# A seven-stage kernel: clearing moved into attention, an early move in the experts stage, free PSUM banks passed on one by one

## The reference, cut to what matters

```
x = x + _layernorm(_L0_attn_ref(_layernorm(x), w_attn, w_proj))          # causal softmax attention, 16 heads of 16
x = x + _layernorm(_L0_ffn_ref(_layernorm(x), ...))                       # 64 experts, 6 a token, at most 96 tokens an expert
x = x + _layernorm(_L1_attn_ref(_layernorm(x), W_qkv, b_qkv, ...))        # linear attention
x = x + _layernorm(_L1_ffn_ref(_layernorm(x), ...))                       # 8 experts, 4 a token, and a shared one

# in _L0_ffn_ref: each expert takes its first CAP = 96 tokens, the rest are dropped
hmid = gelu(einsum('ech,ehf->ecf', xs, w1))
y = einsum('ecf,efh->ech', hmid, w2)
out = zeros((t, h)).at[token_of].add(y_pair)                              # sums over a token's experts
shared = gelu(x @ sw1.T) @ sw2.T
return out + shared

# in _L1_attn_ref, the features of queries and keys
q = elu(q * E ** -0.5) + EPS_FEAT                                         # EPS_FEAT = 1.0001
k = elu(k) + EPS_FEAT
```

## Time and profile before

| | us |
|---|---|
| median of 3 runs | 3391.13 (3386.59 to 3397.05) |
| the profiled execution | 3387.51 |
| its span, first to last instruction | 3385.8 |
| PE busy | 2875.2 (85%) |
| DVE busy | 2228.2 (66%) |
| ACT busy | 1606.3 (47%) |
| POOL busy | 734.7 (22%) |

### The profile page before, as it was taken

The page is one execution under the profiler, slowest core; times in us unless marked ns, Lnnn a source line. Parts: engine busy times, 40 slices in busy tenths (PEclk is TensorE's granted clock), DMA queues, the critical chain, the costliest instruction groups (busy, mean ns, idle before and its releaser), DMA issues. The chain is left out here.

```text
span 3385.8 us, 58986 instructions
## 1 busy us (share of the span) xinstructions
PE 2875.2 (85%) x19969; PEld 2070.7 (61%) x19969; DVE 2228.2 (66%) x6153; ACT 1606.3 (47%) x2398; POOL 734.7 (22%) x876
## 2 busy tenths in 40 slices
PE   6767999999999577574983776999489999999998
PEld 5653444444444266464773664556378888888887
DVE  5448999999999278555335884444366666666664
ACT  2222777777777444331323553455234444444443
POOL 0011222222222133243773441222100000000000
PEclk9886999999999766587996887899689999999999
DMA  6776565656553278684976997554324342425241
GB/s 178 225 209 90 90 99 91 89 85 96 95 92 63 74 251 287 216 332 110 228 185 196 290 288 238 159 174 149 137 72 116 72 116 70 117 69 118 67 102 44
DMA packets 423046, 489.02 MB, mean 144 GB/s; under 512 B 92112, under 2 KB 309232, under 8 KB 420592
## 3 DMA queue, kind: packets, MB, share of 16 engines
q1 hardware_dynamic: 409856, 453.74, 51.6%
q0 software_dynamic: 10240, 14.16, 2.4%
q10 hardware_dynamic: 2800, 19.20, 1.5%
HBM read 280.34 MB, written 206.10 MB: 144 GB/s over the span
## 5 line engine op out<-in xcount | busy, mean ns | idle before, releaser
L529 ACT ACTIVATE att_pr<-att_e_ps 128x1024 f32<-128x1024 f32 (+2 forms) x640 | 567.2, 938 | 203.2 <-PE att_e_ps L581 203.2
L557 PE MATMUL att_m_ps<-att_ks,att_qs 63*128 63x512 f32 (+3 forms) x1536 | 466.2, 433 | 41.1 <-PEq L39 32.5
L491 DVE CUSTOM_DVE_ANT_0 att_kept<-att_m_ps,att_causal 128x256 f32<-128x256 f32 (+3 forms) x1024 | 448.5, 488 | 48.6 <-DVEq L39 21.9
L557 PEld LDWEIGHTS att_m_ps<-att_ks,att_qs 63*128 63x128 f32 x1536 | 234.7, 189 | 371.5 <-DVE att_mx L494 148.0
L494 DVE TENSOR_REDUCE att_mx<-att_m_ps 128x1 f32<-128x512 f32 x512 | 323.4, 684 | 21.4 <-PE att_m_ps L557 17.4
L470 POOL TENSOR_SCALAR_AFFINE_SELECT att_pr<-att_pr 128x256 f32<-128x256 f32 (+1 forms) x384 | 181.2, 484 | 698.0 <-PEq L572 694.5
L601 PE MATMUL att_o_ps<-att_pr,att_vs 128*32 128x512 f32 (+3 forms) x3072 | 328.7, 501 | 3.7 <-issue 1.9
L2574 ACT ACTIVATE fin_hh<-fin_hid 128x512 fp32r<-128x512 f32 x192 | 121.4, 632 | 400.4 <-DVE fin_hid L2420 299.7
L581 PE MATMUL att_e_ps<-att_qs,att_ks 64*128 64x512 f32 (+3 forms) x1536 | 269.4, 377 | 4.8 <-ACT att_pr L529 2.9
L2313 POOL TENSOR_TENSOR fin_rs<-fin_ve,fin_mhalf 128x4 f32<-128x4 f32 x48 | 48.4, 1007 | 928.4 <-POOLq L39 928.4
L2416 DVE TENSOR_TENSOR fin_hid<-fin_gate,fin_u_ps 128x512 f32<-128x512 f32 x192 | 131.7, 686 | 138.0 <-ACT fin_gate L2568 82.9
(11 more groups left out here) (331 smaller groups left out, 6966.1 us busy)
## 6 DMA issues: line engine op xcount, KB each, us to landing
fin_raw<-weights SPq DMA_DIRECT2D x32, 1024.0 KB, 12.7
att_qs<-q_high SPq DMA_DIRECT2D x128, 128.0 KB, 5.1
att_ks<-k_high SPq DMA_DIRECT2D x128, 128.0 KB, 6.7
attended<-att_ot SPq DMA_DIRECT2D x64, 256.0 KB, 2.0
moe_w<-w SPq DMA_DIRECT2D x128, 128.0 KB, 3.4
acc<-moe_zero ACTq DMA_DIRECT2D x16, 1024.0 KB, 12.0
lqk_a<-acc SPq DMA_DIRECT2D x32, 512.0 KB, 6.2
attended<-lin_ot SPq DMA_DIRECT2D x32, 512.0 KB, 3.5
```

The source lines that it names most:

```text
L491: e.tensor_tensor_reduce(kept[:, n % MBUF, 0:w], m_ps[:, n % MBUF, 0:w], causal[:, BLK - w:], 1.0, -3e38, ALU.add, ALU.max, mx[:, h, at, q ...
L529: e.activation(out, src, ACT.Exp).then_inc(exp_done, 1)
L557: e.matmul(m_ps[:, (2 * i + n) % MBUF, 0:w], qs[rows, j, p, q * P:(q + 1) * P], ks[rows, j, p, h * BLK:h * BLK + w], start=True, stop=True ...
```

## The change

Five edits, in four stages.

1. First stage: SyncE signals `qk_read` for each bank as soon as that bank's low part is ready, waits for the values, signals `v_read`, and only then issues all eight stores. TensorE waits for one bank at a time.
2. Attention: a block of zeros is filled by GpSimd, and SyncE issues two stores of 256 KB to `acc0` and `acc1` after each group's row; it waits for all of them at the stage's end.
3. Experts stage: ScalarE's 16 clearing stores are gone, only the three small ones for the dummy rows stay. The small move is issued after 16 pieces and not after 44. VectorE splits the second weight behind `pack()` and not before it.
4. Experts stage, pairs: VectorE's `low` for a pair's second and later pieces comes behind the next pair's `xt` copy.
5. Input of linear attention: `phi = max(qk + bias + 1.0001, min(ex, 1) + 1e-4)`. `ex` is clamped two banks at a time in SBUF; the step that makes `phi` reads PSUM.

```
@@ phase_qkv, sync
                         j = b[1]
-                        e.wait_ge(ol_ready, 4)
+                        for c in range(4):
+                            e.wait_ge(ol_ready, c + 1)
+                            e.sem_inc(qk_read, 1)
+                        e.wait_ge(vo_ready, 1)
+                        e.sem_inc(v_read, 1)
                         for d, s, c in ((qh_d, oh, 0), (kh_d, oh, 2), (ql_d, ol, 0), (kl_d, ol, 2)):
                             e.dma_start(...).then_inc(stored[j], 16)
-                        e.sem_inc(qk_read, 1)
-                        e.wait_ge(vo_ready, 1)
-                        e.sem_inc(v_read, 1)
@@ phase_qkv, tensor
-                        e.wait_ge(qk_read, 1)
                         for c in range(4):
+                            e.wait_ge(qk_read, c + 1)
@@ phase_softmax_attention
+        ZERO = N // G // P * C
+        zero = ph.sb("zero", [P, ZERO])
+        zero_rows = [d[0:N].rearrange("(g p r) c -> g p (r c)", g=G, p=P) for d in zeroed]
+                def clear(g):
+                    for rows in zero_rows:
+                        e.dma_start(rows[g], zero[:]).then_inc(zeros_stored, 16)
                     if more:
                         row(nxt)
+                    clear(g)
@@ phase_shared_and_experts, sync
-                for k in range(ALONE):
+                for k in range(MOVE):
                     follow(k)
                 e.wait_ge(local_ready, 1)
                 e.dma_start(both[:, 1], val[E0:P]).then_inc(moved, 16)
+                for k in range(MOVE, ALONE):
+                    follow(k)
@@ vector
+                split(0, w1h, w1l, w1f)
                 e.wait_ge(choice_loaded, 32)
                 e.wait_ge(iotas_ready, 2)
                 pack()
+                split(1, w2h, w2l, w2f)
                 largest(val[:], key[:])
...
+                    if n:
+                        for k in pieces(n - 1)[1:]:
+                            low(k)
                     low(ks[0])
-                    low(ks[1])
...
-                    for k in ks[2:]:
-                        low(k)
@@ scalar
                 for k in range(ALONE):
                     follow(k)
-                    if k < 2 * (N // (P * ZR)):
-                        n, a = k // 2, k % 2
-                        e.dma_start(zero_v[a][n], zero[:]).then_inc(zeros_stored, 16)
@@ phase_linear_qkv, vector
-                                begun.append(step.begin(e.tensor_scalar(re[:, k], qk[:, k], bqke[:, k:k + 1], FE,
-                                                                        ALU.add, ALU.max)))
-                                e.scalar_tensor_tensor(phi[:, j, k - 1], ex[:, k - 1], 1.0, re[:, k - 1], ALU.min,
-                                                       ALU.add).then_inc(phi_done, 1)
+                        for half in (slice(0, 2), slice(2, 4)):
+                            e.wait_ge(exp_ready, half.stop)
+                            step(e.tensor_scalar(ex[:, half], ex[:, half], 1.0, FE, ALU.min, ALU.add))
+                            for k in range(half.start, half.stop):
+                                e.scalar_tensor_tensor(phi[:, j, k], qk[:, k], bqk1[:, k:k + 1], ex[:, k], ALU.add,
+                                                       ALU.max).then_inc(phi_done, 1)
```

More of the change, by code:

```diff
@@ L254, in _ @@
             def _(e):
-                e.sem_inc(qk_read, 1)
+                e.sem_inc(qk_read, 4)
                 e.sem_inc(v_read, 1)
@@ L267, in stages @@
                                     (lambda k: xh[:, j, k], lambda k: xl[:, j, k]), KC).then_inc(qk_ready, 1)
-                        take(e, (xl_ready, 1), (qk_read, 1))
+                        take(e, (xl_ready, 1), (qk_read, 4))
                     if a is not None:
@@ L317, in phase_softmax_attention @@
         o_ps = ph.ps("o_ps", [P, BLK])
+        zero_ready = ph.sem("zero_ready")
+        zeros_stored = ph.sem("zeros_stored")
         first_ones = ph.sem("first_ones")
@@ L436, in _ @@
                 row(1)
+                e.wait_ge(zero_ready, 1)
+                clear(0)
                 with e.Fori(0, LOOPS) as i:
@@ L442, in _ @@
                 outputs(G - 1, 1)
+                e.wait_ge(zeros_stored, 16 * len(zeroed) * G)
             @block.gpsimd
@@ L459, in _ @@
                 e.sem_inc(later_ones, 1)
+                step(e.memset(zero[:], 0.0))
+                e.sem_inc(zero_ready, 1)
                 step.close()
@@ L1150, in phase_shared_and_experts @@
     ON_POOL = 6
+    MOVE = 4 * NF
     REST = 2 * NF * NB - ALONE
@@ L1244, in phase_shared_and_experts @@
         sh_v = sh_d.rearrange("(b j t p) c -> b j p t c", j=2, t=TPB, p=P)
-        ZR = 2048 // C
-        zero_v = [d[0:N].rearrange("(n p r) c -> n p (r c)", p=P, r=ZR) for d in accs]
-        ZEROS = 2 * (N // (P * ZR)) + 3
         with nc.Block() as block:
@@ L1361, in unpack, with split @@
                         step(e.scalar_tensor_tensor(left[:], bit[:], -weight, left[:], ALU.mult, ALU.add))
-                for n, (high, low, full) in enumerate(((w1h, w1l, w1f), (w2h, w2l, w2f))):
+                def split(n, high, low, full):
                     e.wait_ge(w_high, n + 1)
@@ L1407, in _ @@
                                         None, ALU.mult).then_inc(scaled, 1)
-                    for k in ks[2:]:
-                        low(k)
+                for k in pieces(PAIRS - 1)[1:]:
+                    low(k)
             @block.scalar
@@ L1528, in phase_linear_qkv @@
         bqk = ph.sb("bqk", [P, 4])
-        bqke = ph.sb("bqke", [P, 4])
+        bqk1 = ph.sb("bqk1", [P, 4])
         bv = ph.sb("bv", [P, C])
@@ L1669, in _ @@
                 step(e.tensor_scalar(bqk[:, 0:2], bqk[:, 0:2], HD ** -0.5, None, ALU.mult))
-                step(e.tensor_scalar(bqke[:], bqk[:], FE, None, ALU.add))
+                step(e.tensor_scalar(bqk1[:], bqk[:], 1.0 + FE, None, ALU.add))
                 e.sem_inc(bias_ready, 1)
@@ L1695, in stages @@
                         j = c[1]
-                        begun = []
-                        for k in range(5):
-                            if k < 4:
-                                e.wait_ge(exp_ready, k + 1)
-                                begun.append(step.begin(e.tensor_scalar(re[:, k], qk[:, k], bqke[:, k:k + 1], FE,
-                                                                        ALU.add, ALU.max)))
-                            if k:
-                                step.done(begun[k - 1])
-                                e.scalar_tensor_tensor(phi[:, j, k - 1], ex[:, k - 1], 1.0, re[:, k - 1], ALU.min,
-                                                       ALU.add).then_inc(phi_done, 1)
+                        for half in (slice(0, 2), slice(2, 4)):
[4 more added lines that the diff above has]
+                                                       ALU.max).then_inc(phi_done, 1)
                         e.wait_ge(v_ready, 1)
```

13 lines of the change are left out of this document (6 added, 7 removed).

## The result

The changed kernel takes 3310.8 us, the median of 4 runs (3300.5 to 3321.1), against 3394.1 before (4 runs): a ratio of 0.9755, interval 0.9716 to 0.9793. The prediction was 3279, with a range to 3310. So the sign was right, the gain is 83 us in place of 115, and the time lies 0.8 us outside the range.

What follows compares the result with a forecast made beforehand. Stages have different limits: a semaphore behind four issues holds the first stage, VectorE's list sets the expert pairs' start. 3387.5 - 51.5 - 0 - 42 - 7 - 8 = 3279.0 us; range 3257 to 3310.

Steps and rivals of the forecast that it cites:

- First stage: First stage: SyncE's earlier bank signals shorten a block from 14.1 to 10.5 us; net -51.5 us, bounds -36.5 and -62.5.
- (c): First stage: transfers take 10.5 us a block, the largest of three near bounds, with 11.0 as upper bound.
- Rival A: First stage: transfers need 11.0 us plus a 1.0 restart, 12.0 a block; gain 29 us, time 3301; chance 0.13.
- The first stage's end: First stage: the last block's stores start after the values copy and not before it, costing 2.5 us.
- Clock: First stage: closing the pauses keeps TensorE's clock fast, mean above 0.95, 9.3 us a block; were it wrong, 11.0.
- Rival B: First stage: the clock does not come back; 11.2 us a block, gain 41 us, time 3289.5; chance 0.13.
- Attention: Attention: the added stores of zeros fit in a hole behind the row; 0 us, at most 42 us slower.
- rival D: Attention: clearing delays the next output, making the kernel slower; at 6 us a group, time 3471; chance 0.02.
- Experts, front: Experts stage before the pairs: clearing removed and move early, so the list is done sooner; -42 us, bounds -36 and -47.
- Rival C: Experts stage, front: the move isn't early, the list ends at 1541.3; gain 18 us, time 3303; chance 0.08.
- Pairs: Expert pairs: copying turned rows earlier returns most of TensorE's 9.7 us of waits; -7 us, bounds 0 and -10.
- Linear input: Input of linear attention: the new phi takes 4.2 us a block, before 5.05; -8 us, bounds 0 and -16.

Runs made afterwards that it cites:

- the wide layout: The changed kernel with values stored in packets of 1088 bytes in place of 272, attention loading from the new places: 3273.6 us, ratio 0.9648.
- the wide packets: The changed kernel with values stored in 1088-byte packets, attention still loading from the old places (only times count): first stage 159.9 us.

## Why the prediction was right or wrong

*First stage: wrong, the one step that decided.* It failed at (c), the transfers. The prediction set three near bounds side by side (9.3 for TensorE, 9.75 for SyncE, 10.5 for transfers) and took the largest. The first is borne out: with one DMA for the values the block is 9.3 us and TensorE is busy throughout. The second fits the 9.6 us of the wide layout, though no run isolates it. The third was 11.8 to 12.2. It called 11.0 us of packet time "the upper bound", since a share of 1 is not the capacity. In the saturated stage the share stands at 1.01 to 1.06, and the packet time of a block is 12.2 to 12.7 us. The values' issues, taken as 4.0 us, were not their cost: the packets went on behind the last issue at a share of 1.38 and 169 GB/s, which stood in the earlier trace rows and was read only as proof that there was room. The Trainium skill's rule on 512 bytes, stated above, would have named the risk: values are stored in pieces of 4 heads x 17 numbers, 272 bytes.

Rival A had the size (12.0 us a block, 3301), but partly by luck. It took the 11.0 us of share as what the engines need and added a restart of 1 us; the packet time was longer than 11.0, and there was no restart, since no microsecond from 40 to 190 us stands empty. Its gain of 29 us is what six profiles give (29.4).

*The first stage's end.* I charged 2.5 us for stores that start later. From TensorE's last matmul to attention's first it took 38.3 and 37.3 us, and 35.7 to 37.9 in the four other profiles of this stage; before, 32.5. That is 3 to 6 us longer. With packets of 544 or 1088 bytes it is 29.3 to 31.6: the same small packets drain there.

*Clock.* The granted clock rose to 0.92 only (40 to 150 us), with pauses before the blocks still there; with no pause it reads 1.00. Rival B described the state, but it was a result of the transfers and not the bound: the wide packets alone brought the clock to 1.00.

*Attention: right*, 0, and rival D had nothing to it: 9.2 us of slack behind the two issues.

*Experts, front: right*, -42 forecast, -43.0 measured: the move 1455.75 - 1397.5 = 58 us after the table's load was issued (61 forecast), the list 95 (96). Port waits cost 4 us where I had 2; the local values being ready 2 us sooner and the move landing in 1.9 us in place of 2.9 made up for it. The rule that I had named from the Trainium skill ("SBUF — State Buffer", section "Who interferes with whom") held, with 1.25 us against 0.20. Rival C's case, a late move, is what the run with the move undone shows: a gain of 22 us in place of 18.

*Pairs: wrong*, -7 forecast, +2 in the first profile, -1 in the mean and none by the run with the order undone. The step that failed is the return of TensorE's 9.7 us of waits for the copy. The prediction had noted that GpSimd's transfers are nearly as long as a pair, and took 7 of the 9.7 all the same. With the earlier copy GpSimd's waits for the weighting fell from 14.4 us to 5.0 (5.2 to 9.9 in the other profiles), but little of that came back: its own issues grew from 150 to 154 us and its waits for landings from 15.3 to 21.5 (9.7 to 19.8 in the others). Why its issues grew is not shown.

*Linear input: right*, -8 forecast, -11.5 in the table, about -6 by the run with it undone.

The sum with the two failed terms set right is 3387.5 - 29 - 42 - 8 = 3308.5. That it lies within 3 us of the median is in part chance: the profiled execution from which the sums start is 6.6 us below the median before (3394.1), and linear attention alone scatters by more than that. The range was too narrow on the upper side: it reached past each rival alone, and two misses in the same direction (the transfers, the pairs) came together with the low start.

## What to carry to other kernels

When the wait that holds a loop is removed, read the cost of its transfers from the stretch where the queue is full, GB/s beside share: a share above 1 at 150 to 250 GB/s, against 400 elsewhere, was small packets at their limit here and not spare room. Then the packet size is the next edit, and worth 28 us here in the blocks; ahead of the change it was worth nothing there.

A wait that moves from one name to another (the copy to the gather) is a sign that the edit removed no bound; undo the edit alone before crediting it. And a stage that scatters by 7 us needs its samples counted: kernels edited elsewhere supply them for nothing.

## What the runs showed of the hardware

The x load's issue took 0.40 us in the kernel before and with wide packets, and up to 3.9 us where the DMA engines were saturated, with everything behind it on that engine, signals too. With 2048 packets of 272 bytes in a block's 3.2 MB the 16 DMA engines carried 260 GB/s, with 1024 of 544 bytes 323. Four DMAs of 128 packets of 1088 bytes took SyncE about as long to issue (3.5 to 4.6 us) as with 272 bytes (4.0), one DMA with the same packets 1.1 us.

Two kernels that differ from the changed one in the first stage alone, by four buffers and a loop of four blocks, had an attention stage of 899.3 and 901.3 us (TensorE's first to last matmul), all others 873 to 876. The trace puts 21.5 us of the first's (21.9 of the second's, 1.2 of the changed kernel's) to waits of TensorE ahead of the products with the values for which no semaphore was late. The DMA queues from 260 to 1100 us show what else differs, the packets that carry instructions. Four buffers, then the changed kernel:

```profile
q8 instruction: 37, 0.61, 0.3%
```

```profile
q8 instruction: 11, 0.18, 0.1%
```

Both long kernels have 37 of these packets of 16 KB there, all fourteen others 10 to 12. TensorE's longest pause ends at such a pair: packets start at 517.2 and 517.8 us, and

```profile
521.76 1.51 PE L637 MATMUL att_o_ps<-att_pr,att_vs 128*32 128x384 f32 x8 [5.09 <-issue]
```

The other pauses of 4.6 to 5.0 us stand in the same way to such packets. So the likely cause is that code of attention's loop is fetched again in its turns, perhaps since the longer first stage moved it to another place; no run tested this.
